# A two-layer AdaLN transformer kernel on one core: local blocks' query and key halves in four PSUM banks, scores per half, refinement on GpSimd, maxima ahead of divisions, new slot orders

## The reference

```
x = x + ga * latent_attention(h)   # h = layernorm(x)*(1+ca)+sa; 8 heads, top-96 of 128 keys:
                                   # 64 local ones, and 32 picked by an index score; keys and values
                                   # gathered per token, softplus rotary parts on queries and keys
x = x + gb * local_transformer(h)  # two layers, each:
    q, k, v = split(shift(x) @ wqkv)            # 8 heads x 64
    q, k = rotary(l2norm(q)*qs), rotary(l2norm(k)*ks)
    o = softmax(8 * q k^T, window of 64) @ v    # blocks of 128 tokens against 128 or 192 keys
    x = x + o @ wo
    h = layernorm(shift(x)) * g + b ;  a, g2 = split(h @ w1 + b1)
    x = x + (a * gelu(g2)) @ w2 + b2
x = x + ga * attention16(h)        # 16 heads x 8, all 256 keys
x = x + gb * moe(h)                # 16 experts, top 8, and a shared one
```

## Time and profile before

| | us |
|---|---|
| median of 3 runs | 1546.39 (1543.72 to 1546.95) |
| profiled execution, its own time | 1545.81 |
| its span, first to last instruction | 1544.0 |
| PE busy | 1352.1 (88%) |
| DVE busy | 926.0 (60%) |
| ACT busy | 862.4 (56%) |
| POOL busy | 324.2 (21%) |

### The profile page before, as it was taken

The page is one execution under the profiler, slowest core; times in us unless marked ns, Lnnn a source line. Parts: engine busy times, 40 slices in busy tenths (PEclk is TensorE's granted clock), DMA queues, the critical chain, the costliest instruction groups (busy, mean ns, idle before and its releaser), DMA issues.

```text
span 1544.0 us, 30598 instructions
## 1 busy us (share of the span) xinstructions
PE 1352.1 (88%) x11816; PEld 966.8 (63%) x11816; DVE 926.0 (60%) x3062; ACT 862.4 (56%) x2231; POOL 324.2 (21%) x420
## 2 busy tenths in 40 slices
PE   5888989898898998988899899888899899888797
PEld 4556657576666566665676566666577567556576
DVE  4755585745565756565366576656446756866634
ACT  3344666554544657545575365754566536665483
POOL 0522030201232211200152112120015310302002
PEclk8989999899999999999999999999999999999999
DMA  8121000000102100000011110000001210000000
GB/s 273 54 61 27 7 1 1 1 4 1 49 21 62 23 5 2 1 1 5 8 42 31 55 23 2 2 1 1 5 8 42 73 24 14 1 1 1 1 1 7
DMA packets 45617, 36.45 MB, mean 24 GB/s; under 512 B 32992, under 2 KB 37536, under 8 KB 44960
## 3 DMA queue, kind: packets, MB, share of 16 engines
q1 hardware_dynamic: 45472, 34.50, 7.8%
HBM read 25.46 MB, written 7.44 MB: 21 GB/s over the span
## 4 chain that ended last, share of the span: by engine, by line
PE 29%; DVE 11%; ACT 7%; issue 2%; POOL 1%; SPq 0%; DMA 0%; POOLq 0%; DVEq 0%; ACTq 0%
PE ps L550 4%; PE ps L757 2%; PE ps L578 2%; ACT arena L1320 2%; PE ps L695 2%; DVE arena L1477 2%; PE ps L743 2%; PE ps L735 2%; DVE small L1726 1%; ACT arena L1114 1%; ACT arena L1268 1%; PE ps L926 1%; PE ps L680 1%; PE ps L1020 1%; PE ps L986 1%
## 5 line engine op out<-in xcount | busy, mean ns | idle before, releaser
L1114 ACT ACTIVATE arena<-ps 128x512 f32<-128x512 f32 (+7 forms) x560 | 251.9, 481 | 229.9 <-PE ps L688 33.2
L550 PE MATMUL ps<-mean_mat 128*128 128x256 bf16 x2038 | 303.4, 282 | 6.8 <-ACT arena L1114 3.4
L550 PEld LDWEIGHTS ps<-mean_mat 128*128 128x128 bf16 x2038 | 192.1, 101 | 97.7 <-issue 55.5
L1901 POOL TENSOR_TENSOR arena<-arena 128x512 f32<-128x512 f32 x64 | 81.3, 1271 | 461.5 <-DVE arena L1497 461.3
L1320 ACT ACTIVATE arena<-arena,small 128x192 f32<-128x192 f32 (+1 forms) x256 | 129.8, 509 | 33.5 <-DVE small L1678 33.0
L1726 DVE TENSOR_REDUCE small<-ps 128x4 f32<-128x1024 f32 x64 | 75.3, 1218 | 25.6 <-PE ps L986 25.3
L1615 DVE TENSOR_TENSOR gath<-ps,rank_tab 96x512 f32<-96x512 f32 x96 | 63.3, 683 | 43.9 <-PE ps L578 43.6
L1779 DVE TENSOR_TENSOR arena<-arena,ps 128x512 f32<-128x512 f32 x64 | 42.8, 686 | 73.1 <-ACT arena L1414 57.9
L1477 DVE CUSTOM_DVE_ANT_0 arena<-ps,mask_w_bf 128x192 f32<-128x192 f32 (+1 forms) x256 | 67.4, 319 | 22.5 <-PE ps L664 22.5
L1370 ACT ACTIVATE arena<-ps 128x512 f32<-128x512 f32 x128 | 66.0, 603 | 23.5 <-PE ps L1020 23.4
L757 PE MATMUL ps<-w_experts,arena 128*128 128x128 f32 x544 | 69.8, 280 | 10.2 <-DVE arena L1779 6.8
(11 more groups left out here) (278 smaller groups left out, 2907.3 us busy)
## 6 DMA issues: line engine op xcount, KB each, us to landing
idxb<-idx_scratch SPq DMA_DIRECT2D x24, 512.0 KB, 5.1
score_scratch<-arena SPq DMA_DIRECT2D x96, 64.0 KB, 1.7
w_experts<-in_experts SPq DMA_DIRECT2D x3, 1088.0 KB, 16.5
w_wqkv<-in_wqkv SPq DMA_DIRECT2D x1, 1536.0 KB, 9.5
arena<-score_scratch SPq DMA_DIRECT2D x96, 16.0 KB, 2.1
arena<-arena SPq DMA_DIRECT2D x96, 16.0 KB, 1.8
arena<-in_x SPq DMA_DIRECT2D x8, 128.0 KB, 2.3
out_x<-arena SPq DMA_DIRECT2D x8, 128.0 KB, 1.9
```

Of the source, the lines that this page charges most:

```text
L550: mm(to, still[:, 0:P], still, start=True, stop=True)
L1114: return act.activation(dst, src, ACT.Copy)
L1901: ins = pool.tensor_tensor(own, own, turned, ALU.add)
```

## The change

The four projections of a layer's queries and keys (two halves) go to four banks at once, the values follow in `bank[0]` and `bank[1]`; `win_scores` of unit 0 needs half 0 alone, and half 1 is transposed in W0 and W1. The Newton step moves from DVE to POOL. In A and W `maxima` stands ahead of `normed` (in A1, A3, A4; A2 keeps the old order). The copies to `xg` and the three transposes go; PE forms the same thing with 64 small matmuls for each image (`turn_gathered`, in A5). The second one-hot tile of the last gather steps is split by rows: two 64-row matmuls for two banks stand beside each other. The rotary query buffers are doubled. The shift of the layer norms in N2 and N3 goes into the bias `b1` (12 matmuls once). `TURNS` and `BUSY` are new throughout: `BUSY` adds up to 1909 fillers, before to 2038. ACT table loads fall from 76 to 68, DMAs that SP issues from 374 to 278.

```diff
-    "pe": ("71222111212151121111121111112121211111211111113121111111111111111111111111112111111111111112111112211111111212"
+    "pe": ("73311114112151213121212111212151111121111112332223211211111121111111111211121111211111111111111111121211112121"
...
-BUSY = [("b0935960007c4ac4135003003811ba0000000201570058454437c00100418390040003500277001305071c906060500620431495211001"
+BUSY = [("10b1081707bc5c3c0192515023070c773006012038911444bc100010221ccc01613403c01b03221085c80c24020055016c0a07c0c04000"
...
-        self.q_tmp = [part(3104 + 256 * i, 256) for i in range(4)]
+        self.q_tmp = [[part(first + 256 * i, 256) for i in range(4)] for first in (7200, 3104)]
...
-                    if name in ("A2", "A4"):
...
-                                sp.dma_start(m.xg[:, n, RANKS * t:RANKS * t + RANKS], src).then_inc(sig(f"xg_loaded{s}"), 16)
...
+                    for i in range(3):
+                        last = mm(bank[g % 2][0:GF, :], m.kv_part[i][:, 0, :], hot[n][:, part], start=(i == 0), stop=(n < 2 and i == 2))
...
+                if n == 2:
+                    for i in range(3):
+                        for g in (2 * p, 2 * p + 1):
...
+                            rows_ = slice(64 * (g % 2), 64 * (g % 2) + 64)
+                            last = mm(bank[g % 2][0:GF, :], m.kv_part[i][rows_, 1, :], hot[3][rows_, part], start=False, stop=(i == 2))
...
+            def turn_gathered():
+
+                pe.wait_ge(*at("u_prob", 4))
+                for h in range(H):
+                    for T in range(2):
+                        rows_, to, n = (slice(LW, P), 0, 16) if T == 0 else (slice(0, P), 16, 32)
+                        for t in range(GP):
+                            last = mm(bank[1][RANKS * t:RANKS * t + RANKS, NG * h + to:NG * h + to + n],
+                                      m.probs_a[T][rows_, h, keys(T):], ident[rows_, rows_.start + t::GP], start=True, stop=True)
+                last.then_inc(*one("xg_turned"))
...
-                    mm(bank[j], m.sh[:, cols(k)], wqkv[:, l, 512 * j:512 * j + 512], start=True, stop=True).then_inc(*one("qk_mm"))
+                    mm(bank[2 * k + j], m.sh[:, cols(k)], wqkv[:, l, 512 * j:512 * j + 512], start=True, stop=True)\
+                        .then_inc(*one("qk_mm"))
...
+                        if i == 0:
+                            pe.wait_ge(*at("qk_parts", 4 * l + 4))
+                            turn_queries(l, 1, 3)
+                        if i == 1:
+                            pe.wait_ge(*at("q_copied", 2 * l + 1))
+                            turn_keys(l, 1, 2)
+                            pe.wait_ge(*at("k_copied", 2 * l + 2))
...
-                else:
-                    act.wait_ge(*at("q_ready", k))
-                    act.wait_ge(*at("q_turned", k))
...
-                        if 0 < i < 5:
-                            n = keys((i - 1) // 2)
-                            probs = m.probs_w[(i - 1) % 3][:, 0:4 * n].rearrange("p (h n) -> p h n", h=4)
-                            normed(1 + l, i - 1, probs, m.tail_w[(i - 1) % 2])
                         if i < 4:
                             dve.wait_ge(*at("u_mm", 4 * l + i + 5))
...
+                            dve.wait_ge(*at("rs_final", 2 * l + i // 2 + 1))
...
+                        if 0 < i < 5:
+                            n = keys((i - 1) // 2)
+                            probs = m.probs_w[(i - 1) % 3][:, 0:4 * n].rearrange("p (h n) -> p h n", h=4)
+                            normed(1 + l, i - 1, probs, m.tail_w[(i - 1) % 2])
...
-                    ln_scaled(2 + l, m.hT, ln_gb[:, l, 0:1], ln_gb[:, l, 1:2])
+                    dve.wait_ge(*at("ln_rstd", 3 + l))
+                    dve.scalar_tensor_tensor(m.hT, bank[1][:, 0:L], ln_gb[:, l, 0:1], m.rstd, ALU.mult, ALU.mult)\
+                       .then_inc(*one("ln_out"))
...
+            def refined(l, k):
+                pool.wait_ge(*at("rs_ready", 2 * l + k + 1))
+                nt, g = newton[s], rs[s][:, k, :]
+                st.link(pool.tensor_tensor(nt, ssq[s][:, k, :], g, ALU.mult))
+                st.link(pool.tensor_tensor(nt, nt, g, ALU.mult))
+                st.link(pool.tensor_scalar(nt, nt, -0.5, 1.5, ALU.mult, ALU.add))
+                st.link(pool.tensor_tensor(g, g, nt, ALU.mult))
```

More of the change, by code:

```diff
@@ L243, in __init__ @@
         self.sq, self.rstd, self.hT = (part(L * i, L) for i in range(3, 6))
[L245 to L247 removed]
+        self.kvsrc = three(1536, NT + 1, GF)
+        self.ckv_b, self.ckv_c = part(1824, DC), part(1856, DC)
+        self.kr_abs, self.kr_raw = three(11552, NT + 1, DR), three(11648, NT + 1, DR)
         self.kaT = part(1920, L)
@@ L252, in __init__ @@
         self.irel = part(3104, 1024)
-        self.q_tmp = [part(3104 + 256 * i, 256) for i in range(4)]
+        self.q_tmp = [[part(first + 256 * i, 256) for i in range(4)] for first in (7200, 3104)]
         self.qi = part(4128, 768)
-        self.qb = three(4128, H, GF)
+        self.qb = [three(first, H, GF) for first in (6176, 4128)]
         self.cqT = part(4896, L, DQ)
@@ L260, in __init__ @@
         self.topb = part(5568, NT * RANKS // 2).bitcast(BF16).rearrange("p (k n) -> p k n", k=NT)
-        self.qa = three(5600, H, DC + DR)
+        self.qa = [three(first, H, DC + DR) for first in (5600, 11744)]
         self.gathT = three(3104, NG, DC)
@@ L268, in __init__ @@
         self.oTa = three(7200, 2, L)
-        self.xg = three(768, 3, P)
         self.og = four(1152, 12, GP, H)
@@ L280, in __init__ @@
         self.squares = [part(9216 + 1024 * k, 1024) for k in range(2)]
-        self.probs_w = [part(5120 + 768 * u, 768) for u in range(3)]
-        self.PTw = [part(7424 + 768 * u, 768) for u in range(2)]
+        self.probs_w = [part(first, 768) for first in (5120, 7168, 6144)]
+        self.PTw = [part(first, 768) for first in (9472, 8192)]
         self.tail_w = [part(8960 + 256 * u, 256) for u in range(2)]
@@ L573, in gather @@
                     part = slice(512 * (g % 4), 512 * (g % 4) + 512)
-                    terms = [(m.kv_part[i][:, 0, :], hot[n][:, part]) for i in range(3)]
-                    if n == 2:
-                        terms += [(m.kv_part[i][:, 1, :], hot[3][:, part]) for i in range(3)]
-                    for i, (l_, r_) in enumerate(terms):
-                        last = mm(bank[g % 2][0:GF, :], l_, r_, start=(i == 0), stop=(i == len(terms) - 1))
-                    last.then_inc(*one("gather_mm"))
+                    for i in range(3):
+                        last = mm(bank[g % 2][0:GF, :], m.kv_part[i][:, 0, :], hot[n][:, part], start=(i == 0), stop=(n < 2 and i == 2))
+                    if n < 2:
+                        last.then_inc(*one("gather_mm"))
+                if n == 2:
+                    for i in range(3):
+                        for g in (2 * p, 2 * p + 1):
+                            part = slice(512 * (g % 4), 512 * (g % 4) + 512)
+                            rows_ = slice(64 * (g % 2), 64 * (g % 2) + 64)
+                            last = mm(bank[g % 2][0:GF, :], m.kv_part[i][rows_, 1, :], hot[3][rows_, part], start=False, stop=(i == 2))
+                            if i == 2:
+                                last.then_inc(*one("gather_mm"))
             def gathered_scores(n):
@@ L854, in tensor_stream @@
                 keep_busy(bank[2][:, 0:L])
-                pe.wait_ge(*at("xg_loaded", 192))
-                for n in range(3):
-                    last = pe.transpose(bank[2][:, cols(n)], m.xg[:, n, :], ident[:, :])
-                last.then_inc(*one("xg_turned"))
                 pe.wait_ge(*at("u_out", 4))
@@ L1257, in scalar_stream @@
                 for i in range(6):
+                    if i == 5:
+                        act.wait_ge(*at("xg_turned", 1))
+                        act.wait_ge(*at("pdiag_zero", 1))
+                        for t in range(GP):
+                            part = slice(RANKS * t, RANKS * t + RANKS)
+                            ins = copy(m.pdiag[part, :, t, :], bank[1][part, 0:H * NG].rearrange("p (h j) -> p j h", j=NG))
+                        ins.then_inc(*one("pdiag_ready"))
                     if i >= 2:
@@ L1273, in scalar_stream @@
                     yield f"A{i}"
-                act.wait_ge(*at("xg_turned", 1))
-                act.wait_ge(*at("pdiag_zero", 1))
-                for t in range(GP):
-                    part = slice(RANKS * t, RANKS * t + RANKS)
-                    ins = copy(m.pdiag[part, :, t, :], bank[2][part, 0:3 * P].rearrange("p (j h) -> p j h", h=H))
-                ins.then_inc(*one("pdiag_ready"))
                 yield "A6"
@@ L1330, in scalar_stream @@
                     yield f"N{2 + l}b"
+                    if r == 0 and l == 0:
+                        act.wait_ge(sig("b1_set"), 2)
                     table(act, ACT.Gelu)
```

268 lines of the change are left out of this document (141 added, 127 removed).

## The result

The changed kernel takes 1554.0 us (median of 8, 1542.2 to 1561.98) where the kernel before took 1545.06 beside it (8 executions, 1541.27 to 1546.95): ratio 1.0057 [1.0032, 1.0082]. It is slower by 0.6%; 1514 was forecast, with a range up to 1550. The profiled execution happens to be the shortest of the eight: 1542.2 us, span 1540.4, at a granted clock of 0.983 where the eight have a median of 0.973. Its rows are used for where work and waits lie, the medians for what the time is.

The account below looks back on a forecast made before the run. The kernel was taken as bound by two chains of dependent steps sharing PE. Terms summed to 32.0 us in the traced half, 64 in the run; half seen gave 1545.8 - 32 = 1514 us, range 1482 to 1550.

Parts of the forecast that it names:

- How much of it is seen: Step from chain gains to time, both streams sharing PE: one half of the 64 us sum shows, giving 1514 us.
- (e): Gathered probabilities by 64 PE matmuls an image, without `xg` copies and transposes: 16.4 us against 8.7, loss 7.7 in traced half.
- (b): Maxima ahead of divisions on DVE in A and W: 1.5 us at 9 places, gain 13.5 in the traced half.
- The slower rival: PE's 27 us of new real work decides if under 0.23 of the other gains is seen; to 1564 us; chance 0.12.
- The rival with a chance of 0.08: PE, not DVE's order, releases the scores; (b), (f), (g) turn into waits on PE: 1545.5 us, no difference; chance 0.08.
- (f): Scores of half 0 before half 1 is transposed: gain 7.5 us in traced half; sign: under 20 us behind first projection.
- (a): Query and key projections in four banks at once, products back to back: 1.8 us at 6 places, gain 10.8 in traced half.
- (c): Newton refinement moved from DVE to POOL, 0.25 us an instruction: gain 1.2 us in traced half, between +5 and -7.
- (d): Split one-hot tile in the gather, L573 about half of L565's time: net 5.7 us in the run, 2.2 in the half.
- (g): Doubled rotary query buffers let half 1 start earlier on POOL: 3 us in the traced half, nothing to 6.3.
- Clock: Fewer fillers could lower the granted clock, each 0.01 costing about 10 us; no case of its own, only room in the range.
- The check on PE: PE's real work becomes 1076 us, 27 more, or 71% of 1514 us, which leaves room, not much.

## Why the prediction was wrong

**The step that failed is "How much of it is seen".** It took one half of the sum, gains and losses alike. The runs show two different shares. A term is missing beside it: `TURNS` is new throughout, and the sum put the new orders at nothing without a reason, where the runs under common orders show that an order moves the same code by 53 to 78 us.

*PE's new work is seen in full.* (e)'s records were sized well in the sum: 27.8 us in the run where 8 x 4.1 = 33 was worked out (for an image 1.8 of matmuls and 1.7 of shape changes, where 1.4 and 2.7 were forecast), and leaving 15/16 of them out gives 29 us back. Its other side was too large: the copies and transposes on the chain were put at 8.7 x 2 = 17.4 us for the run. In the kernel before, exchanging them for 14.0 us of small matmuls cost 5.5, so they were worth 8.5. (e) costs 15.4 by my sum, and the half let 7.7 of it count; measured in the old orders it is 1565.04 - 1545.12 = 20 us.

*The gains are hardly seen.* The other terms summed to 79 us. The result is +9 and (e) is +20, so about 11 of the 79 arrived, a share of 0.14. (This takes (e)'s 20 us over from the old orders; on the changed side its gross cost of 29 to 31, less 8.5, is 20.5 to 22.5, which gives 11.5 to 13.5.) The share is an average that has the new orders in it, not a property of each term: (b) is worth 27 where it stands. Whether the missing gains never came or the new orders took them back stays open. The slower rival named 0.23 as the share below which it decides, and by its own sum, 18 for the new work less 0.14 x 79 = 11, it comes to 1553. It had a chance of 0.12, and its time of 1564 set the gains at nothing. Half of its mechanism is shown, that PE's new work counts in full; that the other stream covered what got shorter is not. The rival with a chance of 0.08, that (b) and (f) turn into waits on PE, has its rows too: 22.5 to 81.7 us ahead of the maxima.

Point by point:

- (a) The projections came as forecast: L711 idles 1.6 us, and the chain has eight of its records in a row (1258.76, 3.63 us) without the gap in the earlier trace rows. The four triples of products are not quite back to back: a sum of squares (1.2 us at 1262.68) stands between the second and the third. What this is worth in time wasn't measured alone.
- (b) 27 us of chain were forecast for the run, half of them to be seen. In the changed kernel undoing it costs 27, in the kernel before doing it costs 63; what the whole change has from it can't be told apart from the orders. I took it that PE writes the scores as soon as the last bias is out, and read in the earlier trace rows that DVE waits there for nothing from PE. But PE has the transposes of the last quotients ahead of those scores (1041.82 and 1042.38), and the division stood on DVE while PE was at them. With it gone from that place, DVE waits for PE, and the quotient waits behind. Most of that wait had no row in the trace of before (22.5 us had): it was the time that the moved instructions were hiding. The exponentials did move together, as forecast: ACT's waits for biases fell from 33.5 to 9.7 us.
- (c) 0.23 us for an instruction on POOL, against 0.25. Alone, in the old orders, it gives 4 us where 2.4 were forecast for the run.
- (d) L573 takes 13.6/96 = 0.142 us where L565 takes 0.248, more than half of it. `idxb` fell from 44.3 to 37.4 us, 6.9 where 5.7 was forecast.
- (e) 3.5 us an image against 4.1. There are no sixteen gaps; the records are longer instead.
- (f) In PE's timeline the first scores behind the projection at 1258.76 start at 1268.61, 9.9 us later (those at 1275.76 on the chain are the second unit's). This is the shortest of 16 such stretches: they run from 9.9 to 32.4 us with a median of 17.6, before from 15.7 to 23.1 with 19.3. Under 20 was no sign of the change, since 11 of 16 were so before and 10 are now; the mean fell by 0.8 us.

```profile
1268.61 0.71 PE L671 MATMUL ps<-arena 64*128 64x128 f32 x8
```

- (g) The place of the earlier trace rows, at 1159, lies ahead of where the chain after begins, so the chain can't tell. In POOL's timeline the second half's block starts 9.1 to 16.4 us behind the first's, before 11.5 to 22.5. Its worth wasn't measured alone.
- Clock: medians of 0.973 with the change and 0.972 before (72 executions beside the experiments), so it doesn't explain the loss.

The check on PE, real work 27 us up, came out at 19, partly by luck: the 27 counted as work some 22 us of shape changes that (e) itself took for idling, and without them, and with (d) at the 11.1 of its own records, the same sum comes to no increase. The changes lie inside the records after all. It was also beside the point: the question was not whether PE has room but whether it stands in the loop.

## What to carry over

In a program whose engines follow written orders, the worth of an edit belongs to the edit and the program around it together: the same swap of two DVE steps cost 63 us in one kernel and gained 27 in the other. A set of new orders is a term of its own in a forecast. Before a step is moved ahead of another, ask what the wait in front of it is that the other step hides, and who waits for the step that now comes later. Here work added to the engine in the loop counted in full and the gains elsewhere at a small share (0.14 on average, in this one case). Small matmuls were cheapest in one shape.

## Of the hardware

- Here a change between small matmuls of 64 and of 128 rows cost 0.11 to 0.14 us of time (128 changes 14.4 us, 112 changes 15.4), and shows inside the matmuls' records (27.8 us against 14.8), not as idle time.
- The time goes with the granted clock from execution to execution. A straight line over the 8 of the changed kernel, 0.964 to 0.983, has -10 us for 0.01, and the eight lie close to it; over 72 of the kernel before, 0.964 to 0.979, it has -3, with a wide scatter. Which of the two drives the other is not shown. The changed kernel is also the less steady one, 1542 to 1562 us.
- A short DVE instruction can still be held up for the length of a 512-column instruction on POOL, and ends with it (598.80 + 1.26 = 600.06, where the first of POOL's two additions ends):

```profile
598.78 2.48 POOL L1938 TENSOR_TENSOR arena<-arena 128x512 f32<-128x512 f32 x2
598.80 1.26 DVE L1709 SCALAR_TENSOR_TENSOR small<-small 128x4 f32<-128x4 f32 x1
L1709 DVE SCALAR_TENSOR_TENSOR small<-small x64: 161/164/1261, 147.1 to 1414.0; 128x4 f32<-128x4 f32 x64
```

  The last row has the shortest, median and longest duration in ns, of the changed kernel.
